# The second layer's output projection moved into its feed-forward, block by block, with W1 and W_o split at the ends of the attentions

## What is computed

```python
# layer 1 (layer 0 before it is like it, without the norms, with relu and D = 512 hidden)
q = layernorm(q_x, ln_q_g, ln_q_b) @ Wq.T
kv = layernorm(kv_x, ln_kv_g, ln_kv_b) @ Wkv.T
attn = softmax(einsum('bhqd,bhkd->bhqk', q, k) * scale)
out = einsum('bhqk,bhkd->bhqd', attn, v)     # 4096 x 512
x = q_x + out @ Wo.T + bo                    # Wo 512 x 512
h = silu(x @ W1.T + b1)                      # W1 2048 x 512
x = x + h @ W2.T + b2                        # W2 512 x 2048
```

## Time and profile before

| | us |
|---|---|
| three runs | 6017.01, 6007.33, 5998.8 |
| median | 6007.33 |
| the profiled execution, its time | 6018.56 |
| its span in the trace | 6016.6 |
| mean granted TensorE clock in it | 0.956 |

### The profile page before, as it was taken

How to read it: one execution, slowest core, us unless ns; L and a number is a source line. 1 busy time by engine, 2 the same in 40 slices (tenths; PEclk the granted TensorE clock), 3 DMA queues, 4 the chain that set the end, 5 groups by cost and what they waited for, 6 DMA issues and landing times. The chain is left out here.

```text
span 6016.6 us, 104478 instructions
## 1 busy us (share of the span) xinstructions
PE 5513.0 (92%) x28932; PEld 3458.3 (57%) x28932; DVE 3760.4 (63%) x6550; ACT 3171.1 (53%) x5833; POOL 2621.9 (44%) x1284
## 2 busy tenths in 40 slices
PE   5959999999979979999999999999999995489999
PEld 4834444444437746666565656656566663367877
DVE  4448887778846667777777777777777773511111
ACT  3327776667743346666666666666666662122222
POOL 0000000000000049999999999999999992000000
PEclk9969998999989989999999999999999997799999
DMA  3441111111124321111111111111111115710000
GB/s 107 119 110 29 32 35 32 33 32 36 28 78 124 107 65 40 39 29 38 40 40 40 39 38 30 40 38 39 41 40 28 40 26 161 237 37 14 28 28 14
DMA packets 322981, 323.19 MB, mean 54 GB/s; under 512 B 183136, under 2 KB 187104, under 8 KB 320480
## 3 DMA queue, kind: packets, MB, share of 16 engines
q1 hardware_dynamic: 322528, 317.82, 20.1%
HBM read 210.79 MB, written 106.82 MB: 53 GB/s over the span
## 5 line engine op out<-in xcount | busy, mean ns | idle before, releaser
L750 DVE TENSOR_REDUCE a_maxes<-a_mscore 128x1 f32<-128x458 f32 (+4 forms) x5632 | 3052.8, 605 | 1031.1 <-PE a_mscore L787 1025.7
L733 ACT ACTIVATE a_prob<-a_score 128x512 f32<-128x512 f32 x4992 | 2595.9, 604 | 1402.2 <-PE a_score L796 1391.0
L787 PE MATMUL a_mscore<-a_k,a_qm 96*128 96x458 f32 (+4 forms) x5632 | 2074.6, 416 | 68.8 <-DMA a_k<-k 56.4
L796 PE MATMUL a_score<-a_q,a_k 97*128 97x512 f32 (+1 forms) x4992 | 2061.9, 436 | 76.4 <-ACT a_prob L733 51.8
L703 POOL TENSOR_TENSOR a_added<-a_added,a_prob 128x1024 f32<-128x1024 f32 x768 | 1831.9, 2385 | 90.5 <-ACT a_prob L733 34.1
L787 PEld LDWEIGHTS a_mscore<-a_k,a_qm 96*128 96x128 f32 (+1 forms) x5632 | 1577.7, 309 | 213.8 <-DVE a_maxes L750 92.5
L815 PE MATMUL a_acc<-a_prob,a_v 128*32 128x512 f32 x9984 | 1617.6, 611 | 0.0
L796 PEld LDWEIGHTS a_score<-a_q,a_k 97*128 97x128 f32 (+1 forms) x4992 | 948.9, 194 | 1133.8 <-ACT a_prob L733 599.1
L700 POOL TENSOR_TENSOR a_added<-a_prob 128x1024 f32<-128x1024 f32 x128 | 304.6, 2380 | 2267.6 <-ACT a_prob L733 2267.3
L810 PE MATMUL a_acc<-a_prob,a_ones 128*1 128x512 f32 x2048 | 965.2, 593 | 0.0
L1118 DVE TENSOR_TENSOR f_hl<-f_h,f_hh 128x512 fp32r<-128x512 f32 x128 | 88.6, 692 | 588.0 <-ACT f_hh L1097 588.0
(11 more groups left out here) (183 smaller groups left out, 3842.9 us busy)
## 6 DMA issues: line engine op xcount, KB each, us to landing
a_qm<-q SPq DMA_DIRECT2D x384, 64.0 KB, 1.9
a_q<-q SPq DMA_DIRECT2D x384, 64.0 KB, 1.9
acc<-a_acc_sb SPq DMA_DIRECT2D x384, 64.0 KB
o_part<-acc SPq DMA_DIRECT2D x24, 1024.0 KB, 10.8
a_k<-k SPq DMA_DIRECT2D x48, 416.0 KB, 5.8
q<-m_qout SPq DMA_DIRECT2D x128, 128.0 KB, 2.3
k<-kv_out SPq DMA_DIRECT2D x30, 512.0 KB, 2.7
a_qm<-q SPq DMA_DIRECT2D x384, 32.0 KB, 1.8
```

The lines of the kernel that those rows point to most:

```text
L733: act.activation(prob[:, t], score[SCORES[it.j][t]][:], ACT.Exp, scale=SCALE).then_inc(exp_done, 1)
L750: dve.tensor_reduce(maxes[j][:, t, c:c + 1], mscore[u % UNIT_BANKS][:, 0:wide], AX.X, ALU.max).then_inc(unit_read, 1)
L787: pe.matmul(mscore[u % UNIT_BANKS][:, 0:wide], qm[j][r:r + ROW, t:NB:NB // P], kt[kk][r:r + ROW, at:at + wide], start=True, stop=True).the ...
L796: pe.matmul(score[SCORES[it.j][t]][:], kt[it.k][r:r + C, i * P:(i + 1) * P], qt[it.j][r:r + C, :], start=True, stop=True).then_inc(score_d ...
```

## The change

Two phases of layer 1, `output_projection` and `feed_forward`, become one, `ending`, which has no `mid` in DRAM and is written out over the 8 blocks without loops. In block n, behind hidden tiles 10 to 13 (`A_AT`), PE makes the 12 matmuls of one output tile of block n+1's output projection (`attended`). DVE and ACT sum, scale and split block n+1's attention result one feature tile at a time, at hidden tiles 1 to 8 (`SUM_AT`, `HALF_AT`), in a single tile `part`. DVE adds bias and x into `X` at tiles 11 to 14 (`ADD_AT`). The split of `X` (`xh`, `xl`, now one buffer each) stands at the block's end.

The weights are prepared elsewhere. In a1, SP loads W1 whole (4 MB) ahead of the first `move_row`, and DVE splits it in place (4 `tensor_copy` and 4 subtractions of 128x2048) when its last maxima are done. It stays in SBUF. In a0 the same is done with W_o (1 MB), and SP then stores its two halves to a DRAM tensor `wo_split` in 8 DMAs behind the last store of the phase (`keep`). `ending` loads these halves back for every block in quarters of 512 KB into two buffers. W2 is loaded and split within block 0 of `ending`, through the four tiles of `X[1]`.

```diff
-def attention(nc, name, H, hd, q, k, v, row, acc_out, sums_out):
+def attention(nc, name, H, hd, q, k, v, row, acc_out, sums_out, weights=(), keep=()):
...
+            for dram, whole, _, _ in weights:
+                sp.dma_start(whole, dram).then_inc(w_loaded, 16)
             move_row(0, 0, 0)
...
+            for to, half in keep:
+                sp.wait_ge(w_lo, len(weights))
+                sp.dma_start(to, f32(half)).then_inc(w_kept, 16)
             for j in range(2):
                 sp.wait_ge(acc_stored[j], H * (QB // 2) * STORED)
+            sp.wait_ge(w_kept, 16 * len(keep))
...
+            if weights:
+                dve.wait_ge(w_loaded, 16 * len(weights))
+            for i, (_, whole, hi, lo) in enumerate(weights):
+                dve.tensor_copy(hi, whole).then_inc(w_hi, 1)
+                dve.wait_ge(w_hi, i + 1)
+                dve.tensor_tensor(lo, whole, f32(hi), ALU.subtract).then_inc(w_lo, 1)
+            if weights:
+                dve.wait_ge(w_lo, len(weights))
...
-def output_projection(nc, name, acc, sums, recips, x, wo, bo, out):
+def ending(nc, name, acc, sums, recips, x, wo_split, bo, W1, b1, func, w2, b2, out):
...
         recips.append(scratch(f"recips{i}", [H, T]))
-    x1, mid = scratch("x1", [D, T]), scratch("mid", [D, T])
+    x1 = scratch("x1", [D, T])
     row = scratch("row", [2, NB])
     ctx_t, x = a["ctx_1024"], a["x"]
@@ -1600,13 +1625,25 @@
             ln=(a["L1_xattn_ln_kv_g"], a["L1_xattn_ln_kv_b"]),
             places={"pe": (0.15, 0.55), "dve": (0.2, 0.4, 0.6, 0.9), "act": (0.2, 0.6, 0.9)})
     project(nc, "pq0", x, T, {"q0": a["L0_xattn_W_q"]}, [("raw", "q0", "items", q[0])])
-    attention(nc, "a0", *L0, q[0], k[0], v[0], row, acc[0], sums[0])
+    wo_split = scratch("wo_split", [KT, 2, P, KT, P])
+    with ExitStack() as ctx:
+        WO = weight(nc, ctx, "wo", KT, D)
+        whole = ctx.enter_context(nc.sbuf_tensor("wo_whole", [P, KT, D], F32))
+        attention(nc, "a0", *L0, q[0], k[0], v[0], row, acc[0], sums[0],
+                  [(a["L1_xattn_Wo"].rearrange("(k p) c -> p k c", p=P), whole[:], WO[0][:], WO[1][:])],
+                  [(wo_split[d, i], WO[i][:, :, d * P:(d + 1) * P]) for d in range(KT) for i in range(2)])
     middle(nc, "m", acc[0], sums[0], recips[0], x, a["L0_xattn_W_o"], a["L0_xattn_w1"], a["L0_xattn_b1"],
            a["L0_xattn_w2"], a["L0_xattn_b2"], a["L1_xattn_ln_q_g"], a["L1_xattn_ln_q_b"], a["L1_xattn_Wq"], x1, q[1])
-    attention(nc, "a1", *L1, q[1], k[1], v[1], row, acc[1], sums[1])
-    output_projection(nc, "o1", acc[1], sums[1], recips[1], x1, a["L1_xattn_Wo"], a["L1_xattn_bo"], mid)
-    feed_forward(nc, "f1", mid, a["L1_xattn_W1"], a["L1_xattn_b1"], ACT.Silu, a["L1_xattn_W2"], a["L1_xattn_b2"], out)
+    with ExitStack() as outer:
+        W1 = weight(nc, outer, "w1", KT, a["L1_xattn_W1"].shape[1])
+        with ExitStack() as inner:
+            whole = inner.enter_context(nc.sbuf_tensor("w1_whole", [P, KT, a["L1_xattn_W1"].shape[1]], F32))
+            attention(nc, "a1", *L1, q[1], k[1], v[1], row, acc[1], sums[1],
+                      [(src, whole[:, i, :], W1[0][:, i, :], W1[1][:, i, :])
+                       for i, src in enumerate(rows(a["L1_xattn_W1"], a["L1_xattn_W1"].shape[1]))])
+        ending(nc, "e", acc[1], sums[1], recips[1], x1, wo_split, a["L1_xattn_bo"], W1, a["L1_xattn_b1"], ACT.Silu,
+               a["L1_xattn_W2"], a["L1_xattn_b2"], out)
```

340 lines of the change are left out of this document (135 added, 205 removed).

## The result

The changed kernel takes **5899.06 us** (median of four runs, 5896.67 to 5907.33); the kernel before, timed between them on the same chip, takes 6003.07 (5998.51 to 6017.01). The ratio is 0.9829, with a 95% interval of 0.9812 to 0.9846. On 6003 us that is 103 less, between 92 and 113. The prediction was 5895 (5872 to 5924). The profiled execution took 5899.1 us, its span is 5897.3, its mean granted clock 0.966.

A forecast was written before the change was run, and what follows sets the result against it. The feed-forward was taken as bound by PE's pace, with the winnable time ahead of it. `ending` at 863.8 for 999.1 us (-135.3), W_o's stores (+9) and W1's split (+14.1) gave -112.2, so 5895 us, range 5872 to 5924.

The forecast's parts named there:

- What goes: The old output projection and feed-forward, from 5017.54 to 6016.6, which the change replaces: 999.1 us.
- The start: From the first DMA of `ending` to its first hidden tile, a chain of loads, reciprocals, splits and projection: 54.3 us.
- a cold spell: PE's slower pace after idling 4.3 us ahead of the first hidden tile: between 0 and 2.7 us, taken as 1.6.
- The blocks: The eight blocks of `ending` at PE's pace: 101.1 us for block 0, 101.5 for six with a 0.4 stall, 89.9 last.
- the first sum comes late: Rival, blocks of `ending`: the 0.4 us stall becomes 4 or more in each of six, +22, 5917 us; chance 0.18.
- W_o's stores: At a0's end, eight stores of W_o's halves behind the last store, not hidden: +9 us.
- The lower end: W_o's stores at a0's end priced as 2.1 MB at 385 GB/s: 5.4 us.
- price of short runs: In W_o's stores, 1.3 ns a run, 0.5 us for 512 runs, from two DMAs of 256 KB.
- W1's load: At a1's start, W1 lands at about 2168.6, before the first `move_row` at 2172.62: 0 us, at most 3.
- W1's split beside POOL: At a1's end, DVE's four CASTs and four subtractions keep POOL out for their whole length: +14.1 us.
- The rival that POOL isn't held: At a1's end, DVE's split of W1 costs POOL nothing: 14.1 us less, 5881 us; chance 0.25.
- The total: Whole kernel: -135.3 for `ending`, +9 for W_o's stores, +14.1 for W1's split, -112.2 us in all.

The follow-up runs named there:

- Experiment 5: Changed kernel, with DVE's reciprocal in `ending` put ahead of the wait for the three bias loads; 5893.1 us, ratio 0.9819 to the kernel before.
- Experiment 4: Changed kernel, with the next block but one's first attention piece loaded before SP waits for the block's output; 5882.76 us, ratio 0.9794 to the kernel before.
- Experiment 3: Changed kernel, with the eight stores of W_o's halves issued ahead of the last item's store in a0; 5898.67 us, ratio 0.9816 to the kernel before.
- experiment 6: Changed kernel, with W_o's halves stored in two transfers of 8 KB runs, quarters read in two transfers each; 5895.76 us, ratio 0.9824 to the kernel before.
- experiment 1: Changed kernel, with W1's rounding (on ACT) and subtraction (on DVE) moved from a1's end to the start of `ending`; 5904.73 us, ratio 0.9830 to the kernel before.
- experiment 2: Changed kernel, with only W1's four subtractions moved to `ending`, the four CASTs staying at a1's end; 5900.82 us, ratio 0.9825 to the kernel before.

## Why the prediction was right

- **What goes, 999.1 us:** as predicted, since the stretch was read, not estimated.
- **The start, 54.3 and a cold spell of 1.6:** 55.64 and 1.6 (the first 24 hidden matmuls took 7.18 in place of 24 x 0.2333 = 5.6, a row within block 0). Inside, two errors cancelled, which is luck. The constants landed at 8.9, not 7; and the store of the reciprocals didn't find the queue busy: it landed 2.4 us behind its issue, not 5. Experiment 5 shows what the predicted wait looks like when it does occur.
- **The blocks, 101.1 and 101.5:** block 0 took 102.4 with the 1.6 in it, the six others 617.2 in place of 609.0. The mechanism was right and the place too. The mis-sized term is the landing of the first piece: 15.5 us after the block's start, not 14.2, since 2 MB took 4.4 us behind the last issue, not 3.1. DVE's split of tile 2 was therefore ready at 18.2, PE wanted it at 16.8, and the stall was 1.5 in place of 0.4. In the sixth block the output's store landed after 5.87 us in place of 3.98, the stall was 3.35 and PE came back at a lower pace, 12 matmuls in 4.60. Experiment 4 puts the price of the whole wait at 14.9 us. It is the mechanism of the rival "the first sum comes late", at a third of the 22 us that were given to it.
- **W_o's stores, +9:** 8.2. Experiment 3 shows that they cost it by place. The lower end, 5.4 by bytes alone, is what experiment 6 measured with long runs, 5.5. The prediction's price of short runs, taken from two far rows, was right in kind: 0.91 us for each 256 KB in place of 0.62. The Trainium skill (DMA: Bandwidth & Descriptors, Specifications) would have the 512-byte runs cost no more than long ones; the traces don't bear that out, with 287 GB/s from DMA engines that are busy throughout.
- **W1's load, 0, at most 3:** about 1.5. The row's first move took 3.19 us in place of 1.42 from store to load (2163.11 to 2166.30), because W1's transfers were still under way: the last landed at 2166.1, 19.5 us behind its issue and 28.9 behind the phase's first load, where the prediction had 22. W1's own megabytes land 2.5 us apart, as fast as it was reckoned; the 4 MB of queries, keys and values ahead of them took 19 us, half the speed that the sum gave them. All eleven executions with the change have it: W1 landed after 28.4 to 29.9 us, and the row's first move took 3.0 to 3.6.
- **W1's split beside POOL, +14.1:** 10.9, and experiment 1 shows that it is DVE's pass and nothing else. By the Trainium skill (SBUF — State Buffer, SBUF: two separate sides) the lock shuts POOL out for each whole instruction; the traces agree that both kinds of operation cost POOL time, a CAST at its double pace included, but not that they cost it their whole length. A CAST of 1.22 us made one of POOL's operations 0.8 to 1.0 us longer, a subtraction of 2.29 us made one 1.8 to 1.9 longer (experiment 2). This is the mis-sized term: 3.4 + 7.5 for the full 14.1. DVE's own operations last longer as well, a subtraction up to 4.36 us; how much of such a record is waiting, the traces don't say. The rival that POOL isn't held is ruled out.
- **The total:** -112.2 predicted, -106 in stretches, -103 by the ratio. The errors are +8.5 in `ending`, -3.2, -0.8 and +1.5, so a split of W1 that was priced too high hid a third of what `ending` was priced too low.

## What to carry to other kernels

When work is moved under an "idle" engine, ask which engine it shares memory with and who ends last there: W1's split cost 11 us beside POOL's last additions, and nothing that shows some 40 us later, with the copies on ACT, while both engines wait for loads. The length of the runs is part of a store's price: 2 MB at a phase's end cost 8.2 us in runs of 512 bytes, 5.5 in runs of 8 KB, and nothing 14 us earlier. A wait in one engine's program holds up all that is queued behind it, so a load on which a block's second third depends must not stand behind the store of the block before. And making the head of a chain earlier gives nothing while a bulk load is still ahead of its next transfer on the same queue: move both, or neither.

## What the runs showed that was not expected

- A CAST of 128 x 2048 takes 1.22 us in the first attention, where POOL has no work, and 2.28 to 3.40 beside it. The subtraction next to it takes 2.29 and there up to 4.36. From the timeline of DVE in the first attention:

```profile
1686.11 1.22 DVE L789 CAST wo_hi<-wo_whole 128x2048 fp32r<-128x2048 f32 x1
1687.36 2.29 DVE L791 TENSOR_TENSOR wo_lo<-wo_whole,wo_hi 128x2048 fp32r<-128x2048 f32 x1
```

- The same small store landed 1.9, 2.4 or 8.9 us behind its issue, by what had been asked for just ahead of it.
- The output's store that is issued in the sixth block took 5.87 us and those in the others 3.98. It does so in all eleven executions with the change, 5.4 to 6.4 us, whatever the order of loads; why, no run says.
- Executions of identical instructions differ by up to 24 us in the first attention's loop (1250.1 to 1274.0 us, clock 0.99 and 0.97), which is more than any single edit here but the change itself.
